# Two attention prologues written as one order each, with the maxima of step 1 moved ahead

## The reference, cut to what matters

```python
qkv = x @ w_qkv
s_loc = einsum('bnihd,bnjhd->bnhij', qw, kw) * scale   # window of 128
s_dil = einsum('bighd,bjghd->bghij', qd, kd) * scale   # every fourth
s_glb = einsum('bihd,bjhd->bhij', q, k) * scale        # all
o = (o_loc + o_dil + o_glb) * (1.0 / 3.0)
...
scores = where(causal, einsum('bhqd,bhkd->bhqk', rope(q), rope(k)) / sqrt(8), -inf)
o = softmax(scores) @ v
```

## Time and profile before

| | us |
|---|---|
| median of 3 runs (lowest to highest) | 1601.72 (1600.91 to 1602.95) |
| profiled execution, its own time | 1599.95 |
| span of that execution in the trace | 1598.2 |
| PE busy | 1377.7 (86%) |
| DVE busy | 1068.3 (67%) |
| ACT busy | 894.7 (56%) |
| POOL busy | 654.2 (41%) |

### The profile page before, as it was taken

One profiled execution on the slowest core, in us unless ns is written; L12 is line 12 of the kernel. 1 busy time (PEld: TensorE's weight loads), 2 busy tenths in 40 slices (PEclk: granted clock), 3 DMA queues, 4 the chain that ended last, 5 costly groups with the idle time before them and its releaser, 6 DMA issues. The chain is left out here.

```text
span 1598.2 us, 36810 instructions
## 1 busy us (share of the span) xinstructions
PE 1377.7 (86%) x12519; PEld 924.5 (58%) x12646; DVE 1068.3 (67%) x2710; ACT 894.7 (56%) x1594; POOL 654.2 (41%) x984
## 2 busy tenths in 40 slices
PE   2799999999999997998999972899999999944866
PEld 1255555555555554766999971355555555534866
DVE  4678778787877763674444444677787887844656
ACT  1567676767767665622444430366666666632666
POOL 2223332323333222055333326656667553342736
PEclk8699999999999998999999995799999999976978
DMA  4211212112121102350111113333433222205653
GB/s 128 66 42 38 59 41 63 53 37 63 35 59 43 62 6 92 90 85 14 49 50 48 49 33 55 84 82 70 113 79 102 71 89 72 68 35 157 213 144 106
DMA packets 91848, 113.65 MB, mean 71 GB/s; under 512 B 13075, under 2 KB 75570, under 8 KB 91538
## 3 DMA queue, kind: packets, MB, share of 16 engines
q1 hardware_dynamic: 74930, 89.74, 19.9%
q0 software_dynamic: 16736, 21.55, 5.7%
HBM read 71.78 MB, written 38.95 MB: 69 GB/s over the span
## 5 line engine op out<-in xcount | busy, mean ns | idle before, releaser
L522 DVE TENSOR_REDUCE wm<-wsm 128x16 f32<-128x512 f32 x512 | 330.1, 685 | 112.4 <-PE wsm L770 109.5
L956 ACT ACTIVATE we<-wst 128x1024 f32<-128x1024 f32 x320 | 325.1, 1023 | 119.9 <-PE wst L803 109.1
L518 DVE TENSOR_REDUCE cnm<-csm 128x1 f32<-128x512 f32 (+3 forms) x352 | 213.8, 637 | 49.4 <-PE csm L767 47.2
L956 ACT ACTIVATE ce<-cst 128x896 f32<-128x896 f32 (+1 forms) x256 | 173.7, 699 | 113.9 <-PE cst L798 75.5
L770 PE MATMUL wsm<-wks,wqs 96*128 96x512 bf16 x512 | 172.1, 391 | 9.8 <-DVE wm L522 6.2
L763 PE MATMUL csm<-cks,cqs 96*128 96x256 bf16 (+3 forms) x512 | 131.8, 309 | 13.8 <-DVE cnm L518 10.1
L803 PE MATMUL wst<-wqs,wks 128*128 128x512 bf16 x417 | 128.3, 383 | 13.3 <-issue 12.0
L2033 PE MATMUL abup<-abxt,abws 128*128 128x128 f32 x1120 | 138.5, 278 | 0.4 <-ACT abxt L2059 0.4
L2033 PEld LDWEIGHTS abup<-abxt,abws 128*128 128x128 f32 x1120 | 132.4, 194 | 0.7 <-ACT abxt L2059 0.7
L837 PE MATMUL woa<-we,wv 128*32 128x128 f32 (+2 forms) x2560 | 130.5, 340 | 0.0
L1058 POOL TENSOR_TENSOR wdif<-wglb,wloc 128x16 f32<-128x16 f32 x32 | 7.1, 221 | 289.7 <-DVE wloc L544 289.7
(11 more groups left out here) (330 smaller groups left out, 3012.3 us busy)
## 6 DMA issues: line engine op xcount, KB each, us to landing
wqs<-qk_parts SPq DMA_DIRECT2D x96, 96.0 KB
wks<-qk_parts SPq DMA_DIRECT2D x96, 96.0 KB
cqs<-qk_parts SPq DMA_DIRECT2D x96, 96.0 KB
cks<-qk_parts SPq DMA_DIRECT2D x96, 96.0 KB
b1r<-rows SPq DMA_DIRECT2D x39, 194.0 KB, 2.7
qk_parts<-wpt SPq DMA_DIRECT2D x48, 128.0 KB
qk_parts<-cpt SPq DMA_DIRECT2D x48, 128.0 KB
b0r<-rows SPq DMA_DIRECT2D x39, 130.0 KB, 2.5
```

Source lines behind the costliest of these rows:

```text
L518: dve.tensor_reduce(NM[:, n % 2, first:first + heads, t], got, AX.X, ALU.max).then_inc(s_mx, 1)
L522: dve.tensor_reduce(M[:, n % 2, hs, t, :].rearrange("p (w f) -> p w f", f=DIL), SM[:, j % 2, :].rearrange("p (w i f) -> p w f i", w=NT, f= ...
L956: act.activation(E[:, e_slot(g, i), 0:width], ST[:, (U * g + i) % 2, 0:width], ACT.Exp, scale=SCALE).then_inc(s_ex, 1)
```

## The change: what it does

`chain` and the lists built from it are replaced by two tuples of events, one for W and one for C, which are taken as the prologue. Against the order before:

- W, batch 0: on ACT `part2(0,0)` comes ahead of `proj(0,1)`. On DVE `left2(0,0)` comes ahead of `left1(0,1)`, and `norm_stats(1)` comes ahead of `left2(0,1)` and of `ones(0,1)`, the memset of the stacked K.
- W, maxima: `smax(1,0)` to `smax(1,4)` stand between `maxima(0)` and `rows(0)`; `smax(1,5)` to `smax(1,11)` stand after it. Twelve units of step 1 are in the prologue, not ten.
- C, batches 0 and 1: on POOL `early(1,0)` (four DMAs) comes ahead of `norm_rows(0)`. On ACT `values(0,0)` comes ahead of `part2(0,1)`, and `part2(1,0)` ahead of `part1(1,1)`. On SP `parts_out(1,1)` comes after `rows(0)`.
- C, maxima: `smax(1,0)` stands ahead of `maxima(0)`, `smax(1,1)` and `smax(1,2)` between it and `rows(0)`, `smax(1,3)` to `smax(1,9)` after it. Ten units of step 1 are in the prologue, not eight.
- Slot 0 of both takes its units of `smax` by numbers of its own (FIRST): 14 in W in place of 16, 9 in C in place of 11. The slots from 1 on are as before.

```diff
+PROLOGUE_W = (("xT", 0), ("norm_stats", 0), ("norm_rows", 0), ("fill", 0), ("ones", 0, 0), ("proj", 0, 0),
+     ("part1", 0, 0), ("part2", 0, 0), ("proj", 0, 1), ("part1", 0, 1), ("left1", 0, 0), ("left2", 0, 0),
+     ("left1", 0, 1), ("part2", 0, 1), ("parts_out", 0, 0), ("norm_stats", 1), ("parts_out", 0, 1),
+     ("left2", 0, 1), ("ones", 0, 1), ("stacks", 0, 0), ("stacks", 0, 1), ("stacks", 0, 2), ("values", 0, 0),
+     ("values", 0, 1), ("norm_rows", 1), ("xT", 1), ("vcopy", 0, 0), ("vcopy", 0, 1), ("proj", 1, 0),
...
+     ("smax", 0, 12), ("smax", 0, 13), ("smax", 0, 14), ("smax", 0, 15), ("maxima", 0), ("smax", 1, 0),
+     ("smax", 1, 1), ("smax", 1, 2), ("smax", 1, 3), ("smax", 1, 4), ("rows", 0), ("smax", 1, 5),
+     ("smax", 1, 6), ("smax", 1, 7), ("smax", 1, 8), ("smax", 1, 9), ("smax", 1, 10), ("smax", 1, 11))
+PROLOGUE_C = (("early", 0, 0), ("ones", 0, 0), ("ones", 0, 1), ("early", 0, 1), ("norm_stats", 0), ("early", 1, 0),
+     ("norm_rows", 0), ("xT", 0), ("proj", 0, 0), ("early", 1, 1), ("fill", 0), ("rot", 0, 0), ("join", 0, 0),
+     ("part1", 0, 0), ("proj", 0, 1), ("part1", 0, 1), ("rot", 0, 1), ("join", 0, 1), ("left1", 0, 0),
+     ("part2", 0, 0), ("left1", 0, 1), ("values", 0, 0), ("part2", 0, 1), ("left2", 0, 0), ("parts_out", 0, 0),
...
+     ("join", 1, 0), ("part1", 1, 0), ("part2", 1, 0), ("proj", 1, 1), ("rot", 1, 1),
...
+     ("smax", 1, 0), ("maxima", 0), ("smax", 1, 1), ("smax", 1, 2), ("rows", 0), ("left2", 1, 1),
+     ("parts_out", 1, 1), ("early", 2, 0), ("smax", 1, 3), ("smax", 1, 4), ("smax", 1, 5), ("smax", 1, 6),
+     ("smax", 1, 7), ("smax", 1, 8), ("smax", 1, 9))
...
+    FIRST = (0, 3, 0, 2, 1, 1, 2, 0) if causal else (1, 2, 2, 0, 2, 0, 2, 2, 1, 2)
...
-                top = []
-                if i < CUT and n + 1 < SLOTS:
+                if n == 0:
+                    units = [("smax", 1 + k // SMU, k % SMU) for k in range(SMU + AHEAD - sum(FIRST[i:]), SMU + AHEAD - sum(FIRST[i + 1:]))]
+                    top = units
+                else:
+                    top = []
+                if n and i < CUT and n + 1 < SLOTS:
                     top = [("smax", n + 1, AHEAD + sum(LATE[:i]) + j) for j in range(LATE[i])]
-                if i >= CUT and n + 2 < SLOTS:
+                if n and i >= CUT and n + 2 < SLOTS:
...
-        order = [("norm_stats", 0), ("norm_rows", 0), ("xT", 0)]
...
-        order += [("smax", 0, j) for j in range(SMU)]
-        order += [("maxima", 0), ("rows", 0)]
-        order += [("smax", 1, j) for j in range(AHEAD)]
+        order = list(PROLOGUE_C if causal else PROLOGUE_W)
```

More of the change, by code:

```diff
@@ L33 @@
 TILES = [(NT - 1, h, 1) for h in range(HG)] + [(2, h, 1) for h in range(HG)] + [(1, 0, 2), (1, 2, 2), (0, 0, HG)]
+PROLOGUE_W = (("xT", 0), ("norm_stats", 0), ("norm_rows", 0), ("fill", 0), ("ones", 0, 0), ("proj", 0, 0),
[3 more added lines that the diff above has]
+     ("values", 0, 1), ("norm_rows", 1), ("xT", 1), ("vcopy", 0, 0), ("vcopy", 0, 1), ("proj", 1, 0),
+     ("part1", 1, 0), ("proj", 1, 1), ("part1", 1, 1), ("left1", 1, 0), ("part2", 1, 0), ("left1", 1, 1),
+     ("part2", 1, 1), ("left2", 1, 0), ("parts_out", 1, 0), ("left2", 1, 1), ("parts_out", 1, 1), ("marks", 0),
+     ("smax", 0, 0), ("smax", 0, 1), ("smax", 0, 2), ("smax", 0, 3), ("smax", 0, 4), ("smax", 0, 5),
+     ("smax", 0, 6), ("smax", 0, 7), ("smax", 0, 8), ("smax", 0, 9), ("smax", 0, 10), ("smax", 0, 11),
+     ("smax", 0, 12), ("smax", 0, 13), ("smax", 0, 14), ("smax", 0, 15), ("maxima", 0), ("smax", 1, 0),
+     ("smax", 1, 1), ("smax", 1, 2), ("smax", 1, 3), ("smax", 1, 4), ("rows", 0), ("smax", 1, 5),
+     ("smax", 1, 6), ("smax", 1, 7), ("smax", 1, 8), ("smax", 1, 9), ("smax", 1, 10), ("smax", 1, 11))
@@ new lines @@
+PROLOGUE_C = (("early", 0, 0), ("ones", 0, 0), ("ones", 0, 1), ("early", 0, 1), ("norm_stats", 0), ("early", 1, 0),
+     ("norm_rows", 0), ("xT", 0), ("proj", 0, 0), ("early", 1, 1), ("fill", 0), ("rot", 0, 0), ("join", 0, 0),
+     ("part1", 0, 0), ("proj", 0, 1), ("part1", 0, 1), ("rot", 0, 1), ("join", 0, 1), ("left1", 0, 0),
+     ("part2", 0, 0), ("left1", 0, 1), ("values", 0, 0), ("part2", 0, 1), ("left2", 0, 0), ("parts_out", 0, 0),
+     ("left2", 0, 1), ("parts_out", 0, 1), ("stacks", 0, 0), ("stacks", 0, 1), ("stacks", 0, 2),
+     ("vcopy", 0, 0), ("vcopy", 0, 1), ("norm_stats", 1), ("norm_rows", 1), ("xT", 1), ("proj", 1, 0),
+     ("rot", 1, 0), ("join", 1, 0), ("part1", 1, 0), ("part2", 1, 0), ("proj", 1, 1), ("rot", 1, 1),
+     ("join", 1, 1), ("part1", 1, 1), ("left1", 1, 0), ("left1", 1, 1), ("part2", 1, 1), ("left2", 1, 0),
+     ("smax", 0, 0), ("smax", 0, 1), ("smax", 0, 2), ("parts_out", 1, 0), ("smax", 0, 3), ("smax", 0, 4),
+     ("smax", 0, 5), ("smax", 0, 6), ("smax", 0, 7), ("smax", 0, 8), ("smax", 0, 9), ("smax", 0, 10),
+     ("smax", 1, 0), ("maxima", 0), ("smax", 1, 1), ("smax", 1, 2), ("rows", 0), ("left2", 1, 1),
+     ("parts_out", 1, 1), ("early", 2, 0), ("smax", 1, 3), ("smax", 1, 4), ("smax", 1, 5), ("smax", 1, 6),
+     ("smax", 1, 7), ("smax", 1, 8), ("smax", 1, 9))
```

## The result

The time fell from 1601.57 us (median of 6 runs, 1600.52 to 1602.95) to 1594.66 us (median of 6, 1592.68 to 1596.65), a ratio of 0.9956 with an interval of 0.9943 to 0.9969: 6.9 us less, faster. Three more comparisons of the same two kernels gave 0.9964, 0.9961 and 0.9959 (each to about 0.0013), so the gain is 0.4%, some 6.4 us. Forecast were 1597.8 us and 3.9 us of gain, with a range that began at 1595.0. The direction was right, the size was not. The profiled execution took 1595.46 us (span 1593.7); busy times are those of before within 1.1 us on every engine, so what went is waiting and time at the lower clock.

What follows compares the result with a forecast made beforehand. PE was taken to bound the steady slots, untouched by the change; gains lay before slot 1. W 0.0 - 2.4 and C -0.6 - 0.3 - 0.6 gave -3.9 us, so 1597.8 us; 8-in-10 range 1595.0 to 1601.6.

Steps and rivals of the forecast that it cites:

- W, start: W up to the first maxima: later memset and reads offset by earlier batch 1 norm rows; 0.0 us, bounds -1.0 and +1.1.
- W, hole: DVE's 4.70 us idle behind W's maxima of step 0: five reduces fill it, first scores 2.06 us earlier, at 64.2.
- W, slot 0: W's slot 0: 12 reduces before the maxima of step 1, not 16; -2.4 us with the hole, bounds -1.9 and -3.2.
- C, start: C up to the first reduce: batch 0 comes 4.6 us later, batch 1 earlier; -0.6 us, bounds -0.7 and +4.6.
- C, hole and slot 0: C's 1.42 us hole filled by more units, -0.3 us; two units fewer in slot 0, -0.6 us, bounds 0.0 and 1.2.
- The rival of the clock: Refilled hole brings 2.4 GHz by W's first scores: W gains 3.2 us, C some 0.7 more; -5.4, 1596.3 us; chance 0.17.
- Given back: W's first reads land late (+0.5); C's late reads and POOL's queue leave C at 0: 1599.8 us; chance 0.22.
- Reads bound: Stacked reads bound both starts, landing over about 6 us after issue: +4.6 in C, +1.1 in W, 1604.1 us; chance 0.09.

Runs made afterwards that it cites:

- w_start: Kernel before with only W's new order of the start; W's maxima of step 0, slot 0 and all of C as before: ratio 0.9995 (0.9981 to 1.0009).
- the eight profiles and the twelve: All 20 profiles, split by C's first reduce after its first memset: eight at 53.14 to 54.24 us, twelve at 51.12 to 52.39 us.
- c_early: Kernel before, except that POOL issues C's early(1,0) ahead of its half of norm_rows(0): 0.9981 (0.9972 to 0.9990), 3.0 us less.
- `moved`: Kernel after with W's Q-stack memset ahead of the first norm, K's in Q's place, C's batch 2 gathers out of POOL's slot 0: 0.9970 against the kernel before.

## Why the prediction was off, step by step

- **W, start: right.** Forecast 0.0, measured 0.31 us earlier in the profile, and w_start's time is 0.8 us below before (3.0 below to 1.4 above). Two moves that cancel, the reads last; they are usable 5.32 us behind their issue, and 41.8 had assumed 5.28 for before. That is luck in part: the only row the 5.28 leaned on said 5.9. The 2 us between data and semaphore that the prediction set beside it stand in the Trainium skill ("DMA: Bandwidth & Descriptors", "Anatomy of one DMA — SWDGE (gpsimd) path") for DMAs that GpSimd issues, setup included. These reads are SP's, and no run shows when their data were in.
- **W, hole: right.** DVE's idle time was forecast to fall to about 1.2 us (1.31), first scores at 64.2 (64.56, 1.87 us earlier in place of 2.06).
- **W, slot 0: right.** `rows(1)` by 75.0 (74.82), sum -2.4; profile -2.65 at slot 1, times 2.5 to 2.7.
- **C, start: mis-sized.** "-0.6, bounds -0.7 and +4.6". It is -1.4 in the first pair of profiles; over the twenty, the eleven that issue `early(1,0)` first have their first reduce at 51.88 us on average and the nine others at 53.51, -1.6. The 4.6 us of delay of batch 0 came nearly as worked out (4.4) and lay beside the gathers; DVE's chain for batch 0 was shorter than I had made it by taking it over from before and adding 0.4 for `values`. The reads, the bound of +4.6, released nothing: PE started 5.8 us behind the end of their issue straight behind its own `rot(1,1)`.
- **C, hole and slot 0: right way, too large.** -0.9 was forecast. The times can't tell it from nothing; the profiles show -0.6 when slot 1 begins (-0.3 in the hole, as forecast, and -0.3 in slot 0, where -0.6 was) and -0.3 when slot 2 begins, with PE waiting for POOL's masks in between.
- **C, slot 2: the step that was missing**, and that failed the forecast. The sum took everything behind slot 0 as fixed ("Nothing later refers to a fixed time, so a microsecond won before slot 1 is won at the end"), and put what a changed clock there is worth at nothing. In the first pair the same instructions of slot 2 took 1.49 us less, and between the eight profiles and the twelve 2.2 us: a stretch of 3.4 us went from 1.2 to 2.4 GHz, and PE waited 0.3 to 0.5 us less. c_early shows that moving `early(1,0)` does it; why the clock falls only behind a late start stays open. The sum with it: -2.65 in W, -1.4 and -1.35 at the landmark in C is -5.4; the mixture between the attentions took 0.77 us more in that pair (387.15 us before, 387.92 after), which leaves -4.6, and the profiled executions differ by 4.5 (1599.95 and 1595.46). The ratios say 6.4. That fits the averages over the two profiles of before and the four of after: -2.9 us at slot 1 of W, and at C's landmark -4.25 and not -2.75; 7.2 us together, and each ratio is good to about 2 us.
- **The rival of the clock** came nearer in size (-5.4), by luck, since it had the wrong place. It put the earlier clock into slot 0 of W; there PE ran at 0.50 until 67.7 us after the change and until 69.2 before, though the hole was filled.

The Trainium skill ("TensorE: Matmul & The Clock Gate", "Part 1: The HAM clock gate") says that the engine is throttled by default and that activity releases it. The trace agrees in so far as the stretch in C has waits of PE in front of it; but with 1.9 us of waits the clock fell in the kernel before, and with 2.8 it did not in c_early, so that sentence alone would not have told which.

"Given back" had POOL's queue take the rest in C; it took back about 0.3 us, and neither of its other terms came. "Reads bound" is true in W, where they are last by 0.91 us, and its price there stayed hidden as forecast.

## What to carry to other kernels

Before calling everything behind a changed prologue fixed, read the granted clock there: here a stretch at 1.2 GHz that appeared only when the start was one to two microseconds late more than doubled what they were worth, and which executions have it is to be asked of several profiles, not of one. When a long hand-written order is changed at many places, one step may carry nearly all of a part: here four DMA issues moved past two small operations in one queue. And where a memset holds a chain of DMAs, try it on an engine that is idle then, even if it takes twice as long there: here the stage behind it began 1.7 us earlier.

## What the runs showed of the hardware

- A stacked read of W was usable 5.32 to 5.63 us behind the end of the issue of its last part, in the six profiles where DMA was the releaser (the four of the kernel after, `moved`, w_start).
- W has an uncertainty of its own in the clock: in the profile of before PE had 1.00 at 45.3 to 48.7 us and 0.50 again until 69.2; in the second profile of the same kernel 0.50 from 31.3 to 72.2 without a break, and W's slots came 1.1 us later.
- POOL zeroed 32x8192 two-byte elements in 6.92 us and 128x3328 four-byte ones in 2.87 us, 0.85 and 0.86 ns per element of a partition whatever the type. That isn't fixed: 128x2048 four-byte elements took 1.80 us in W and 2.41 us in C.
